# Values turned by VectorE through DRAM, keys scaled on GpSimd, and a new hand-written order, in a gated delta rule kernel

## The reference, cut to what matters

```python
qkvz = (hidden_states @ W_qkvz).reshape(B, S, NK, 2 * DK + 2 * R * DV)
...
conv = sum((xp[:, j:j + S, :] * conv_weight[:, j] for j in range(KCONV)))
mixed = jax.nn.silu(conv)
...
core = _chunk_gated_delta_rule(q, k, v, g, beta)   # l2norm of q and k inside
x = core * jax.nn.silu(z.astype(jnp.float32))
x = x * jax.lax.rsqrt(jnp.mean(x * x, axis=-1, keepdims=True) + EPS) * norm_weight
return x.reshape(B, S, VD) @ W_out
```

## Time and profile before

| | us |
|---|---|
| median of 3 runs | 4418.93 (4417.82 to 4419.18) |
| the profiled execution, own time | 4417.5 |
| its span, first to last instruction | 4415.7 |
| outside the span | 1.8 |

### The profile page before, as it was taken

The page is one execution under the profiler, slowest core; times in us unless marked ns, Lnnn a source line. Parts: engine busy times, 40 slices in busy tenths (PEclk is TensorE's granted clock), DMA queues, the critical chain, the costliest instruction groups (busy, mean ns, idle before and its releaser), DMA issues. The chain is left out here.

```text
span 4415.7 us, 140088 instructions
## 1 busy us (share of the span) xinstructions
PE 4211.2 (95%) x44246; PEld 3699.2 (84%) x44246; DVE 3725.5 (84%) x6642; ACT 3842.3 (87%) x10855; POOL 2334.8 (53%) x3319
## 2 busy tenths in 40 slices
PE   3799999999999999999999999999999999999788
PEld 2688888888888888888888888888888888888645
DVE  5688888888888888888888888888888888888656
ACT  2699999999999999999999999999999999999655
POOL 3355555555555555555555555555555555555444
PEclk9899999999999999999999999999999999999989
DMA  5544444444444443434343434343434444444200
GB/s 183 179 134 143 134 140 134 140 135 140 137 138 142 132 147 128 151 125 153 123 154 121 154 120 154 120 154 121 153 124 150 129 145 133 141 134 141 70 10 29
DMA packets 450786, 584.82 MB, mean 132 GB/s; under 512 B 237472, under 2 KB 315552, under 8 KB 433184
## 3 DMA queue, kind: packets, MB, share of 16 engines
q1 hardware_dynamic: 449568, 575.59, 40.6%
q10 hardware_dynamic: 1152, 8.39, 0.5%
HBM read 533.81 MB, written 50.07 MB: 132 GB/s over the span
## 5 line engine op out<-in xcount | busy, mean ns | idle before, releaser
L1014 DVE SCALAR_TENSOR_TENSOR conv<-ps,cws,conv 128x511 f32<-128x511 f32 (+2 forms) x1536 | 1084.8, 741 | 59.3 <-ACT conv L892 39.3
L698 PE MATMUL ps<-xb,wb 128*128 128x512 f32 x3072 | 841.8, 409 | 26.0 <-DMA wb<-w_scratch 21.7
L698 PEld LDWEIGHTS ps<-xb,wb 128*128 128x128 f32 x3072 | 541.2, 189 | 129.2 <-issue 30.2
L1057 DVE CAST_PREDICATED pl<-masks,ps 128x512 f16<-128x512 uint16 x768 | 546.8, 712 | 55.3 <-PE ps L760 32.6
L953 ACT ACTIVATE t<-ps 128x512 f16<-128x512 f32 x768 | 465.8, 607 | 118.4 <-PE ps L768 107.3
L1263 POOL TENSOR_TENSOR xo<-xo,zs 128x512 f32<-128x512 f32 x128 | 164.0, 1281 | 714.3 <-DVE xo L1108 714.3
L1263 POOL TENSOR_TENSOR xo<-xo,home 128x512 f32<-128x512 f32 x128 | 163.0, 1273 | 699.8 <-DVE xo L1108 699.8
L957 ACT ACTIVATE u<-ps 128x512 f16<-128x512 f32 x768 | 473.1, 616 | 43.6 <-PE ps L773 43.6
L858 PE MATMUL ps<-wo,xt 128*128 128x256 f32 x3072 | 429.4, 289 | 33.4 <-DVE xt L1114 32.6
L712 PE MATMUL ps<-wb,xb 128*128 128x256 f32 x3072 | 428.3, 289 | 0.0
L858 PEld LDWEIGHTS ps<-wo,xt 128*128 128x128 f32 x3072 | 384.6, 191 | 47.4 <-issue 41.9
(11 more groups left out here) (188 smaller groups left out, 11691.8 us busy)
## 6 DMA issues: line engine op xcount, KB each, us to landing
xb<-x_scratch SPq DMA_DIRECT2D x128, 1024.0 KB, 5.8
wb<-w_scratch SPq DMA_DIRECT2D x128, 1024.0 KB, 5.7
decays<-rows_scratch SPq DMA_DIRECT2D x128, 512.0 KB, 3.7
wb<-w_scratch SPq DMA_DIRECT2D x128, 512.0 KB, 4.3
wo<-wout_scratch SPq DMA_DIRECT2D x128, 512.0 KB, 6.3
rk<-rk_scratch SPq DMA_DIRECT2D x128, 256.0 KB, 4.1
w_scratch<-wsplit SPq DMA_DIRECT2D x128, 192.0 KB, 3.2
wpiece<-in_Wqkvz SPq DMA_DIRECT2D x128, 96.0 KB, 2.5
```

The source lines that it names most:

```text
L698: last = nc.tensor.matmul(proj_bank[c][:, :], wb[:, pw, k * WCOL + c * D:k * WCOL + (c + 1) * D], xb[p][:, px, k * S:(k + 1) * S], start=( ...
L1014: nc.vector.scalar_tensor_tensor(out=conv[c][:, back:S], in0=proj_bank[c][:, 0:S - back], scalar=cws[p][:, c * TAPS + 3 - back:c * TAPS + ...
L1057: nc.vector.copy_predicated(halves(pl[l], l, 0), mask[:, None, :, :].broadcast_to([128, NU, C // (4 << l), 2 << l]), packed(p_bank, l)).th ...
```

## The change

- `turn` is left for K and Q alone. The values are turned by `flip_v` on VectorE: two instructions per item transpose 32x32 blocks of `conv[V0]`, `conv[V1]` into `flip`, which shares its place with the decay factors `et`. `store_v` writes it to DRAM (512 KB), and `load_v` reads it back with four loads of 128 KB into `vt`, which puts the blocks in their places. `values` on ScalarE is gone. `residual` reads `vt` through a rearranged view.
- `decay` on ScalarE waits in addition for the store of the item before (`v_out`).
- `keys` moves from VectorE to GpSimd.
- `ORDER` is written anew for all engines, SP included: other offsets (-3 to 2 for -2 to 3), other places. `load_x` and `load_w` are for item + 1 (before: +3 and +2). `out_mm` is for item - 3 in both groups.
- The shared banks are dealt out anew, with other waits.
- `split` and `ws_out` wait for 32 instead of 16. In `feed_forward` the layer norm stages stand at other places in their list.

```diff
+    v_dram = nc.dram_tensor("v_scratch", (128, 4, R * NC * 32), f32, kind="Internal").ap()
-        vt = [home[:, 1, :].rearrange("p (n h d) -> p n h d", n=NC, h=R), sb("vt1", [128, NC, R, D])]
+        vt = [home[:, 1, :].rearrange("p (w x) -> p w x", w=4), sb("vt1", [128, 4, R * NC * 32])]
+        flip = et[:, :, :].rearrange("p (q u) c -> p q (u c)", q=4)
...
-        proj_bank = (ps[5], ps[6], ps[5], ps[6])
-        z_bank = (ps[5], ps[6])
+        proj_bank = (ps[6], ps[7], ps[5], ps[7])
+        z_bank = (ps[6], ps[6])
-        turn_bank = (ps[7], ps[5], ps[7], ps[5])
-        gram_bank = (ps[6], ps[7])
-        o_turn_bank = (ps[7], ps[7])
-        out_bank = (ps[7], ps[7])
+        turn_bank = (ps[6], ps[7], None, None)
+        gram_bank = (ps[6], ps[5])
+        o_turn_bank = (ps[5], ps[5])
+        out_bank = (ps[6], ps[7])
...
+            at(-1, ("z", g1)) + at(-2, ("y_copy", 3)) + at(-1, ("t_mm", 5)) + at(0, ("conv", V1, 2), ("conv", V0, 3)) + at(-1, ("t_copy", 5),
+               ("ff_abs", 0), ("ff_abs", 1)) + at(-2, ("o_rnorm", g0)) + at(-1, ("u_mm", 5), ("u_copy", 5)) + at(0, ("keys", 0))
+            + at(-1, ("load_v", 0), ("ff_load", 2), ("ff_load", 0)) + at(-2, ("o_norm", g0)) + at(0, ("conv", V1, 3)) + at(-2, ("q_part", 3))
+            + at(-3, ("out_mm", g0)) + at(-1, ("resid_mm", g0), ("resid_mm", g1)) + at(-3, ("added", g0)) + at(-1, ("resid", g0))
+            + at(-2, ("intra_mm", 3)) + at(0, ("turn", Q)) + at(-2, ("out", 3), ("ff_below", 2), ("ff_tern", 2)) + at(-1, ("ff_set", 0))
+            + at(1, ("load_x", 0)) + at(0, ("gram", g0)) + at(-2, ("gate", g1)) + at(-1, ("fix_mm", g0), ("resid", g1), ("residual", 0))
+            + at(0, ("decay", g0), ("system", g0), ("squares", Q)) + at(-1, ("fix_mm", g1), ("ff_total", 0)) + at(0, ("decay", g1))
+            + at(-1, ("fix", g0)) + at(0, ("gram", g1), ("attn", g0), ("diagonal", g0), ("system", g1), ("diagonal", g1)) + at(1, ("load_w", 0))
+            + at(-2, ("o_square", g1)) + at(0, ("rounded", g0), ("rnorm", Q)) + at(-3, ("out_mm", g1)) + at(1, ("project", K))
...
+            + at(-1, ("y", 2)) + at(1, ("rnorm", K)) + at(-1, ("y_copy", 2)) + at(0, ("flip", 0), ("t_mm", 3), ("u_mm", 3)) + at(-1, ("qs_mm", 2))
+            + at(0, ("t_copy", 3)) + at(-1, ("update_mm", 2)) + at(0, ("p_mm", 4)) + at(-1, ("q_part", 2)) + at(0, ("flip", 1))
...
+            + at(0, ("z", g0)) + at(-1, ("qs_mm", 3), ("o_square", g0)) + at(1, ("conv", V1, 1)) + at(0, ("low", g1), ("store_v", 0))
+            + at(1, ("store_norm", 0), ("silu", Q)) + at(0, ("p_mm", 5)) + at(-3, ("store_split", 0)) + at(0, ("u_copy", 4), ("project_z", g1))
+            + at(1, ("load_norm", 0)) + at(-1, ("y", 3)) + at(0, ("p", 5)) + at(1, ("conv", V0, 2))
...
+            def store_v(a, p, _):
+                sp.wait_ge(flipped.sem, flipped.at(a, 2))
+                vt_in.wait(sp, a - 1, 64)
+                sp.dma_start(v_dram[:, :, :], flip).then_inc(v_out.sem, 16)
+            def load_v(a, p, _):
+                sp.wait_ge(v_out.sem, v_out.at(a, 16))
+                res_ready.wait(sp, a - 2, NC)
+                for w in range(4):
+                    sp.dma_start(vt[p][:, w, :], v_dram[w * 32:(w + 1) * 32].rearrange("r q x -> q r x")).then_inc(vt_in.sem, 16)
...
-            def values(a, p, h):
-                act.wait_ge(turn_mm.sem, turn_mm.at(a, h + 3))
-                res_ready.wait(act, a - 2, NC)
-                nc.scalar.activation(vt[p][:, :, h, :], four(turn_bank[V0 + h]), ACT.Copy).then_inc(vt_ready.sem, 1)
...
+                v_out.wait(act, a - 1, 16)                    # decay
...
+            def flip_v(a, p, h):
+                ve.wait_ge(silued.sem, silued.at(a, h + 3))
+                attn_ready.wait(ve, a, 2)
+                nc.vector.transpose(flip.rearrange("p q (h n c) -> p h q n c", h=R, n=NC)[:, h],
+                                    conv[V0 + h][:, :].rearrange("p (n q c) -> p q n c", n=NC, q=4)).then_inc(flipped.sem, 1)
...
+                nc.gpsimd.tensor_tensor(kq[p][:, :, 0, :], conv[K][:, :].rearrange("p (n c) -> p n c", n=NC),
+                                        rk[:, :].rearrange("p (c n) -> p n c", n=NC), ALU.mult).then_inc(kq_ready.sem, 1)
```

More of the change, by code:

```diff
@@ L550, in delta_rule @@
         ORDER = (
[L551 to L580, removed]
@@ new lines, in delta_rule @@
+            + at(-1, ("y_copy", 0)) + at(0, ("t_first", g1)) + at(-2, ("x_copy", g0)) + at(0, ("t_first_copy", 1)) + at(-1, ("update_mm", 0))
+            + at(0, ("silu", V0)) + at(-3, ("added", g1)) + at(-1, ("intra_mm", 0)) + at(0, ("t_first_copy", 0)) + at(-2, ("o_norm", g1))
+            + at(0, ("small", 0), ("ff_load", 1), ("load_wz", 0)) + at(-2, ("x_low", g0)) + at(-3, ("split", 0)) + at(-1, ("state", 0),
+               ("ff_halves", 1), ("ff_abs", 2)) + at(0, ("p_mm", 0), ("p", 0)) + at(-2, ("o_turn", g1)) + at(-1, ("out", 0)) + at(1, ("conv", K, 1))
@@ new lines, in delta_rule @@
+            + at(-1, ("y_copy", 1)) + at(0, ("p_mm", 2)) + at(-1, ("q_part", 1)) + at(0, ("u_mm", 1)) + at(-1, ("intra_mm", 1), ("update_mm", 1))
+            + at(0, ("p", 2)) + at(-2, ("load_raw", 0)) + at(0, ("u_copy", 1)) + at(1, ("silu", K)) + at(0, ("t_mm", 2), ("u_mm", 2), ("t_copy", 2))
+            + at(-1, ("out", 1)) + at(0, ("kw", 0)) + at(1, ("turn", K)) + at(-1, ("state", 1)) + at(1, ("key_tokens", 0), ("squares", K))
+            + at(-1, ("ks_mm", 2)) + at(1, ("conv", Q, 3)) + at(2, ("taps", 0)) + at(-1, ("residual", 2), ("ff_below", 1), ("ff_halves", 2))
@@ new lines, in delta_rule @@
+            + at(-1, ("intra_mm", 2)) + at(0, ("t_mm", 4)) + at(1, ("tap", V1)) + at(0, ("t_copy", 4), ("u_mm", 4)) + at(-1, ("gate", g0))
+            + at(1, ("mask_row", g1)) + at(-1, ("out", 2)) + at(1, ("conv", V0, 1)) + at(-1, ("ks_mm", 3), ("residual", 3), ("ff_tern", 1))
+            + at(0, ("z", g0)) + at(-1, ("qs_mm", 3), ("o_square", g0)) + at(1, ("conv", V1, 1)) + at(0, ("low", g1), ("store_v", 0))
+            + at(1, ("store_norm", 0), ("silu", Q)) + at(0, ("p_mm", 5)) + at(-3, ("store_split", 0)) + at(0, ("u_copy", 4), ("project_z", g1))
@@ L675, in ff_load @@
                 sp.dma_start(FF_RAW[q].rearrange("p (k n) -> p k n", k=k), src.rearrange("(k p) n -> p k n", p=128)).then_inc(ff_in[q].sem, 16)
-            steps(sp, ff_load=ff_load, load_w=load_w, load_wz=load_wz, load_x=load_x, load_raw=load_raw, store_split=store_split, load_rows=load_rows, store_norm=store_norm, load_norm=load_norm, load_wout=load_wout)
+            steps(sp, ff_load=ff_load, load_w=load_w, load_wz=load_wz, load_x=load_x, load_raw=load_raw, store_split=store_split, load_rows=load_rows, store_norm=store_norm, load_norm=load_norm, store_v=store_v, load_v=load_v, load_wout=load_wout)
         @block.tensor
```

92 lines of the change are left out of this document (50 added, 42 removed).

## The result

The changed kernel takes 5446.99 us (median, 5434.93 to 5448.72); the kernel before took 4418.38 us beside it. The ratio is 1.232, 95% interval 1.231 to 1.234. The forecast was 4310 us and faster: wrong in sign, and far outside the range.

The account below looks back on a forecast made before the run. TensorE's queue was taken to bound the kernel. From the profiled 4417.5 us, -116.5 for the removed turns and +8 for a stall at the start gave 4309, forecast 4310 us with the run median's 1.4 added; range 4258 to 4400.

Parts of the forecast that it names:

- the X of the part on SP: SP's queue: time from the flips to the landing of load_w, put at 14.0 us.
- I cost it at zero: SP's chain of loads: 15.5 + 14.0 = 29.5 us, under the 30.4 us step, so hidden with 0.9 us to spare.
- K to flips: TensorE from projection K's start to the first flip's place: 14.5 us, with the flips about 15.5.
- us per step: SP's chain: if its cover is gone, each us of X costs one us per step.
- the forecast 30.4: Step length in us expected after the change, against 31.31 before.
- Rival D: SP's chain sets the step, projection K waiting for wb or xb: X 16.7, step 32.2 us, 4534 us; chance 0.11.
- TensorE's 0.91 us per item: TensorE: the removed turns of V0 and V1, 0.44 + 0.47 us per item, 116.5 us over 128 items.
- all of it is on the path: TensorE: the whole 116.5 us of removed turns comes off the kernel's time.
- Rival C: VectorE, at 91% load, comes just in time and delays TensorE's inversion groups: 0.45 us per step, 4368 us; chance 0.22.
- Just covered: GpSimd: keys, at about 1.28 us, is ready in time for gram; its small waits neither gained nor lost.
- The one stall at the start: TensorE waits once, about 10 us, for item 2's projection, less 2 already lost: +8 us (0 to +12).
- Fill and drain are the same within a few us: Start and end of the item phase: number of steps, fill and drain unchanged within a few us.

Follow-up runs that it names:

- run 1: The changed kernel with load_v's four loads cut by 32 destination partitions, so over 16 engines instead of 4: 4736.56 us.
- run 15: run 10 without store_v and load_v; flips stay, vt holds a constant, token-major values left out: 4360.45 us.
- 12 to 15: Four runs; the first is run 1 with each of load_v's four loads cut to a quarter of its bytes, 4448.19 us; then run 13, run 14, run 15.
- run 11: The kernel before, in its own order, without the values' turns and copies and nothing in their place (constant in vt): 4369.73 us, ratio 0.990.
- run 13: run 10 with load_w cut in two, K's 256 KB first on its own semaphore, projection Q waiting for the other 768 KB: 4345.18 us, ratio 0.9851.
- run 4: The kernel before with only keys moved from VectorE to GpSimd: 4444.17 us, ratio 1.0069.
- run 14: run 13 with load_x cut in two by tokens, the first 512 KB issued one step earlier: 4343.63 us.
- run 10: run 1 with load_wz (512 KB) taken out of the burst and issued beside load_raw: 4688.59 us.
- run 8: The kernel before, in its own order, with the values' new path, load_v on 4 engines as the change writes it: 4934.96 us.
- run 5: The kernel before, in its own order, with the values' new path, load_v on 16 engines, keys on VectorE: 4422.99 us, ratio 1.0022.

## Why the prediction was wrong

**The step that failed is the X of the part on SP**, X = 0.1 + 3.7 + 5 x 0.87 + 5.8 = 14.0, and with it "I cost it at zero". The loop that it describes is the right one; two of its terms were mis-sized and one was missing. In the step shown above, the flips end 17.0 us after K starts (15.5 forecast) and X is 21.6. Term by term:

- The store was right, 3.7.
- From the flips' end to `load_w`'s issue it took 9.5 us, 8.15 by the sum. `load_norm` stands ahead of `load_v`, and `load_x` keeps SP for 1.80 us, where it keeps it for 0.36 in run 1.
- The landing was 12.0 us instead of 5.8. Of these 6.2 us the four engines make 3.8 (8.2 in run 1), the values' and z's bytes over 16 engines 0.6 (7.6 in run 15), and 1.8 are there without any values: in run 15 only the megabyte of `xb`, issued 0.7 us ahead, is in the way. The 5.8 belonged to `xb` with 512 KB just ahead of it; `wb` itself had nothing ahead for some 4 us in the kernel before, and its row there is

```profile
wb<-w_scratch SPq DMA_DIRECT2D x128, 1024.0 KB, 5.7
```

- K to flips was taken as fixed. It is 15.7 us in the runs in which K waits about a us or less (12 to 15), 17.1 in run 1 and 17.6 in the change, as means between 1000 and 3500 us: what TensorE does behind the wait runs at the lower clock, 1.24 us of it in K itself. So a us of X costs more than the "us per step" of the forecast.

The mean step of the change is 39.3 us, 17.6 + 21.6, which is 8.9 above the forecast 30.4, and 128 x 8.9 = 1135 us is nearly all of the 1137 missed. `load_v` was priced by its issues alone, as if it were no load on the engines behind it.

**Rival D was right, and was given 0.11.** It is this mechanism by name. Its price, 16.7 for X and 4534 us, had the burst at 0.6 us and a slower store that did not come. X was 21.6 in the change; over 16 engines it is 17.0, close to D's, and the time is still 4737, since K to flips is 17.1 there and not 15.5. I dismissed it over a margin of 0.9 us in a sum with a landing time borrowed from another traffic: "I cost it at zero" should have been a range of some us on either side. D was also missing the term of the clock, by which K to flips grows with K's wait.

**Of the other steps:**

- TensorE's 0.91 us per item: its queue is that much shorter. But "all of it is on the path" fails in the order before, where its removal brings 0.35 us (run 11). In the new order most of run 13's steps without a wait of K's take 30.0 to 30.4 us, near the forecast 30.4 (with half a us of K's wait they are 30.8 us long, from K at 3956.27 to K at 3987.07). That the new list was needed for it is likely, but not shown: no run keeps the values' turns in the new list, so what the list gives by itself is not known, and the agreement may be luck in part.
- VectorE: the flip takes 0.688 us, the forecast 0.68, which was borrowed from an ordinary pass of the same size; that a transpose costs the same was luck. The row, by line and form:

```profile
L1038 DVE STREAM_TRANSPOSE decays<-conv 128x512 f32<-128x512 f32 x256 | 166.3, 688 | 0.0
```

- By the Trainium skill, page "VectorE: DVE Perf Modes", section "The three transpose paths", four tiles of 128x128 in 32x32 blocks would be 4 x 311 ns = 1.24 us, an estimate from its bf16 figure; this trace disagrees with 0.69. Rival C did not come: in run 13 VectorE is at 89% and TensorE hardly waits.
- GpSimd's keys: 1.54 us, not 1.28. "Just covered" holds in run 13 (1.5 us of waits in 1000), not in the old order (run 4, +30 us) and not in run 14.
- The one stall at the start: forecast 10 us. In the change K waits 20.6 us there (at 186 us), in run 13 14.1 us.
- "Fill and drain are the same within a few us" is wrong in run 13. The first and last start of the projections and of `out_mm` there:

```profile
L724 PE MATMUL ps<-xb,wb x3072: 387/396/794, 111.0 to 4032.4; 128*128 128x512 f32 x192
L880 PE MATMUL ps<-wo,xt x3072: 274/283/561, 237.0 to 4135.3; 128*128 128x256 f32 x192
```

and in the kernel before:

```profile
L698 PE MATMUL ps<-xb,wb x3072: 387/396/796, 112.7 to 4117.1; 128*128 128x512 f32 x192
L858 PE MATMUL ps<-wo,xt x3072: 277/282/746, 197.2 to 4199.9; 128*128 128x256 f32 x192
```

From first to last projection run 13 gains 83.0 us (3921.4 against 4004.4). From there to the last `out_mm` it gives back 20.1 (102.9 against 82.8), since `out_mm` is for item - 3. The feed-forward end is 8.1 us shorter (207.7 against 215.8) and the begin 1.7. -83.0 + 20.1 - 8.1 - 1.7 = -72.7, the difference of the spans, 4343.0 and 4415.7. The forecast had 108.5, so with its transfers mended it would still have been 36 us too low: 25.5 from the first to the last projection, which the start (14.1 instead of 10) and K's waits for `wb` (7.7 us per 1000) more than cover, and 20.1 of drain, less the 9.8 gained at the two ends, which it had taken as 0.

What stays open: what holds the old order a third of a us below TensorE's queue (run 11), what the new list gives without the values' new path, and what run 10 would take without `load_w`'s wait for `rk`.

## What to carry to other kernels

Before pricing a transfer, look at the outermost dimension of both sides: a rearrangement that put a 4 there put the transfer on 4 engines here, and every transfer behind it waited on those four. Price a landing by what is in flight at that moment, not by the median of a quiet row (here a megabyte of weights: 5.7 us alone, 7.6 with another megabyte just ahead); list every wait that the issuing queue makes on the way, such as that for `rk` here; and when a load comes just in time, send first the part that the next instruction needs. When all engines lose busy share at once, look for one wait per step and follow it round to the queue that it passes through.

## What the runs showed of the hardware

- Four loads of 128 KB each in 1 KB pieces, with a 4 outermost on one side, are all there 11.6 us after the first issue (the change) and 11.7 (run 8); with 32 outermost on both sides 6.4 (run 1) and 6.5 (run 5). The first kind makes 5 semaphore updates per transfer, the second 16. The 1 MB of `wb` behind the first kind lands in 12.0 instead of 8.2 us.
- The 1 MB of `wb` lands in 5.7 us with nothing just ahead (the kernel before), in 7.6 with another megabyte issued 0.7 us ahead of it (run 15).
- Over 16 engines the burst of run 1 peaks at 387 GB/s, over the stretch in which `load_v`, `load_x` and `load_w` fly.
- After 6.7 us without work TensorE's granted clock is 0.50, and projection K takes 2.92 us instead of 1.64. With K's waits at 68.8 us per 1000 (run 1) the middle stretch is at 0.95, with 7.7 us (run 13) at 1.00.
- GpSimd takes 1.54 us for a f32 product over 512 columns that VectorE does in 1.10, VectorE's 32x32 block transpose of 512 f32 columns 0.688 us.
